# Scaled queries made in the transposed layout, the normalizer folded into the head LayerNorm, and the fill and the first loads moved

## The chip, the cores and the metric

The kernel runs on one core of a Trainium2 chip. The time is device microseconds of one execution, and the number compared is the median of several. A TensorE (PE) multiplies, a VectorE (DVE), a ScalarE (ACT) and a GpSimd (POOL) do the elementwise work, and a SyncE (SP) issues most DMAs. Each engine works through its own list in order, and they wait for each other on semaphores.

## The reference, cut to what matters

Input: `x` and `ctx`, 8 sequences of 512 tokens with 1024 features. Two residual blocks follow each other. The first is an mLSTM attention with 16 heads of 64, whose queries are the layer-normed x and whose keys and values are ctx. The second is a mixture of 16 experts, two per token, with a shared expert.

```python
log_D = log_fg + ig;  max_log_D = max over t;  D = exp(log_D - max_log_D)
C = (q @ k.T / sqrt(64)) * D
normalizer = maximum(abs(C.sum(-1)), exp(-max_log_D))
h = (C / (normalizer + 1e-6)) @ v
hn = (h - mean(h)) * rsqrt(var(h) + 1e-6) * ln_scale      # per head of 64
x1 = x + tanh(g_xattn) * hn
shared = (silu(f @ sg) * (f @ su)) @ sd                   # f: x1, layer-normed
routed = sum over the two best experts e of  w_e * (silu(f @ eg[e]) * (f @ eu[e])) @ ed[e]
out = x1 + tanh(g_ffn) * (shared + routed)
```

## The kernel before

The 4096 tokens are 32 chunks of 128, four to a sequence. There are two blocks, one after the other, with a barrier between them.

**The mix block** (`mix_block`) does, per chunk, both LayerNorms, gates, attention, router and the first half of the shared expert, whose weights stay in memory in a high and a low part (12 pieces, `w_hi` and `w_lo`, made from three staging slots in the first two turns: stage W). A chunk's work is cut into stages (a letter) and parts (a digit). One tuple, `TURN`, gives the order of all stages in a turn, and `OFFSET` says which chunk a stage works on: in the turn of chunk j, stage Q works on j+2, A (gates) and F on j+1, B (attention) on j, C (head LayerNorm) on j-1, D, E, N, G on j-2 and K, U, H, Y, J (shared expert) on j-3. Every engine runs the same tuple and takes from it the stages that it has. `AHEAD` is what comes ahead of the first turn. The first sequence is written out, six are a loop of four turns, and the last is written out with three turns more to drain.

Attention is chunkwise: within a chunk the scores times the decays (`gbd`, made from a row per head that goes to memory as `mid_g_row` and comes back to all 128 partitions), and across chunks a running `state` per head that is multiplied with scaled queries `qs_t`. In the three chunks of a sequence that have one ahead (j > 0), stage F makes `qs_t`: DVE multiplies the queries `q` by a factor per row and head (`qfac`, L674 and L676), PE transposes the product into `p_tr` (8 transposes of 128x128 in two halves, L850) and ACT copies each half out (L502). Stage Q makes the plain transposed queries `q_t` in the same way, from `q` (L626), through the same `p_tr`. Each half waits until the half ahead of it in `p_tr` has been copied out (`tr_before`).

Stage C divides the attention's output by the normalizer (L720 to L722), subtracts the mean per head and squares; the variance gets 1e-6 added (L731), and POOL takes its power -0.5 (L448).

**The expert block** (`ffn_block`) goes through the experts' tiles of 128 tokens (73 in this run), gathered by index, and then through the 32 chunks with the other half of the shared expert. A tile's output goes to `mid_y`, which has room for 98 tiles. The tiles beyond 73 are filled by SP with any finite rows, 25 DMAs from `mid_z` (L1139), between the second expert's weights and the first store of a tile (L1123). ACT can copy a tile's output into `y` (L1261) only when the store of the one before has landed. The last chunk gathers two rows per token (L1220, `r0` and `r1`), waits for them, joins them with the shared expert's half and stores 128 rows at once (L1132).

The kernel starts with seven constant loads, of which DVE, ACT and PE await all (`const_in` 112), then zeroes of the expert lists, then the first rows of x (L318).

## Time and profile before

| | us |
|---|---|
| median of 3 runs | 3263.84 (3263.45 to 3267.43) |
| the profiled execution | 3260.97 |
| its span, first to last instruction | 3259.4 |

| engine | busy us | share of the span |
|---|---|---|
| PE | 3012.4 | 92% |
| DVE | 1681.5 | 52% |
| ACT | 1025.7 | 31% |
| POOL | 609.4 | 19% |

The span has two parts: the mix block up to about 1326 us and the expert block behind it. Shares of the span are means over both, and DVE is busy at about 75 to 80% in the first and under 45% in the second. "Idle before" is the time that an engine stood still ahead of an instruction, and the name behind the arrow is what ended it. The 16 transposes of the plain and the scaled queries have one line, L850, with those of `xn` and `th`.

### The profile page before, as it was taken

The page shows a single profiled execution, that of the slowest core. Times are in us where ns is not written, and L with a number is a line of the kernel's source. Part 1 is how long each engine was busy: PE and PEld are TensorE (multiplying, and loading weights), DVE is VectorE, ACT ScalarE, POOL GpSimd, SP SyncE. Part 2 cuts the span into 40 slices and gives each one's busy share as a digit, 9 for nine tenths or more (in the row PEclk, how much of TensorE's full clock was granted, in tenths as well). Part 3 has the DMA queues.
Part 4 walks back from the last instruction along what each step waited for, and adds up shares of the span by engine and source line. Part 5 has one row for each costly group of instructions (what it writes and reads, how often), then busy time and mean ns, then how long its engine had stood idle before and what let it go on. Part 6 is the DMA issues. An engine that isn't in the chain of part 4 may idle for free.

```text
span 3259.4 us, 50815 instructions
## 1 busy us (share of the span) xinstructions
PE 3012.4 (92%) x17478; PEld 2478.7 (76%) x17479; DVE 1681.5 (52%) x3164; ACT 1025.7 (31%) x1940; POOL 609.4 (19%) x572
## 2 busy tenths in 40 slices
PE   3799998898989998689999999999999999999998
PEld 3677777777777776578888888888888888888886
DVE  3687777787878775323333333333333334444444
ACT  3444443343444331223233333333333321111110
POOL 1233333333333432100000000000000001111111
PEclk9699999999999997799999999999999999999999
DMA  4333333333434321553333442443242234444444
GB/s 151 117 105 121 115 119 116 105 105 107 126 108 123 111 85 46 216 179 140 135 136 135 142 173 103 174 161 114 101 175 100 109 135 152 145 154 137 157 146 133
DMA packets 200706, 424.54 MB, mean 130 GB/s; under 512 B 85472, under 2 KB 85984, under 8 KB 200160
## 3 DMA queue, kind: packets, MB, share of 16 engines
q1 hardware_dynamic: 176160, 349.67, 31.8%
q0 software_dynamic: 24400, 72.96, 6.8%
q8 instruction: 87, 1.43, 0.2%
q14 instruction: 59, 0.48, 0.0%
HBM read 333.42 MB, written 102.27 MB: 134 GB/s over the span
## 4 chain that ended last, share of the span: by engine, by line
PE 54%; DMA 1%; DVE 1%; issue 1%; ACT 1%; SPq 1%; ACTq 0%; POOL 0%; POOLq 0%; DVEq 0%
PE p_g_b L1451 17%; PE p_up_b L1451 17%; PE p_y_b L1439 16%; PE p_x_b L1419 3%; PE p_h_b L1426 1%; DMA mid_y<-y_b 1%; DVE w_lo_b L1294 1%; ACT w_hi_b L1237 1%; SPq L1139 0%; DMA xg_b<-mid_xn,idx_b 0%; DMA r_b<-mid_y,slot_now_b 0%; ACTq L1103 0%; DMA idx_b<-mid_lists 0%; SPq L1138 0%; DVE r_b L1347 0%
## 5 line engine op out<-in xcount | busy, mean ns | idle before, releaser
L1310 DVE TENSOR_TENSOR ht_lo_b<-p_h_b,ht_hi_b 128x512 fp32r<-128x512 f32 x105 | 72.5, 691 | 557.4 <-ACT ht_hi_b L1249 553.4
L1451 PE MATMUL p_g_b<-w_hi_b,xt_hi_b 128*128 128x512 f32 x840 | 339.2, 404 | 20.3 <-DVE w_lo_b L1294 18.4
L1439 PE MATMUL p_y_b<-w_hi_b,ht_hi_b 128*128 128x512 f32 x840 | 336.9, 401 | 6.8 <-DVE ht_lo_b L1310 6.8
L1451 PE MATMUL p_g_b<-w_hi_b,xt_lo_b 128*128 128x512 f32 x840 | 328.9, 391 | 0.0
L1451 PE MATMUL p_up_b<-w_lo_b,xt_hi_b 128*128 128x512 f32 x840 | 328.7, 391 | 0.0
L1451 PE MATMUL p_up_b<-w_hi_b,xt_lo_b 128*128 128x512 f32 x840 | 328.5, 391 | 0.0
L1439 PE MATMUL p_y_b<-w_hi_b,ht_lo_b 128*128 128x512 f32 x840 | 328.1, 391 | 0.0
L1451 PE MATMUL p_up_b<-w_hi_b,xt_hi_b 128*128 128x512 f32 x840 | 328.0, 391 | 0.0
L1439 PE MATMUL p_y_b<-w_lo_b,ht_hi_b 128*128 128x512 f32 x840 | 327.9, 390 | 0.0
L1451 PE MATMUL p_g_b<-w_lo_b,xt_hi_b 128*128 128x512 f32 x840 | 326.8, 389 | 0.0
L1322 DVE SCALAR_TENSOR_TENSOR sg_b<-th_b,p_g_b 128x512 f32<-128x512 f32 x105 | 72.2, 687 | 486.6 <-ACT th_b L1279 486.6
L1294 DVE TENSOR_TENSOR w_lo_b<-stage_b,w_hi_b 128x1024 fp32r<-128x1024 f32 x204 | 234.7, 1220 | 110.2 <-ACT w_hi_b L1244 66.9
L1249 ACT ACTIVATE ht_hi_b<-p_h_b 128x512 fp32r<-128x512 f32 x105 | 62.9, 599 | 558.2 <-PE p_h_b L1426 414.7
L919 PE MATMUL p_g<-w_hi,xt 128*128 128x512 f32 x512 | 221.9, 433 | 15.6 <-issue 14.4
L1190 POOL DMA_INDIRECT xg_b<-mid_xn,idx_b x73 | 71.1, 974 | 827.3 <-PE p_x_b L1419 785.4
L1279 ACT ACTIVATE th_b<-p_g_b 128x512 f32<-128x512 f32 x105 | 63.3, 603 | 512.9 <-PE p_up_b L1451 512.9
L919 PE MATMUL p_up<-w_hi,xt 128*128 128x512 f32 x512 | 209.1, 408 | 0.0
L1451 PEld LDWEIGHTS p_g_b<-w_hi_b,xt_hi_b 128*128 128x128 f32 x840 | 158.1, 188 | 55.6 <-DVE w_lo_b L1294 20.4
L1439 PEld LDWEIGHTS p_y_b<-w_hi_b,ht_hi_b 128*128 128x128 f32 x840 | 158.4, 189 | 36.9 <-DVE ht_lo_b L1310 7.4
L1451 PEld LDWEIGHTS p_g_b<-w_lo_b,xt_hi_b 128*128 128x128 f32 x840 | 158.0, 188 | 34.5
L1451 PEld LDWEIGHTS p_g_b<-w_hi_b,xt_lo_b 128*128 128x128 f32 x840 | 158.0, 188 | 34.2
L1451 PEld LDWEIGHTS p_up_b<-w_lo_b,xt_hi_b 128*128 128x128 f32 x840 | 157.7, 188 | 34.3
(216 smaller groups left out, 5837.5 us busy)
## 6 DMA issues: line engine op xcount, KB each, us to landing
mid_y<-y_b SPq DMA_DIRECT2D x73, 512.0 KB, 3.3
x<-in_x SPq DMA_DIRECT2D x64, 512.0 KB, 3.7
gbd<-mid_g_row SPq DMA_DIRECT2D x64, 512.0 KB, 5.1
stage_b<-in_eg SPq DMA_DIRECT2D x16, 2048.0 KB
stage_b<-in_eu SPq DMA_DIRECT2D x16, 2048.0 KB, 15.2
stage_b<-in_ed SPq DMA_DIRECT2D x16, 2048.0 KB, 19.4
ctx_t<-in_ctx_t SPq DMA_DIRECT2D x32, 512.0 KB, 4.6
ctx_v<-in_ctx SPq DMA_DIRECT2D x32, 512.0 KB, 7.7
```

Of the source, the lines that this page charges most:

```text
L919: last = nc.tensor.matmul(out[:, :], xt[:, a, k, :], w[:, k, o:o + FE], start=(k == 0 and m == 0), stop=(k == KD - 1 and m == 2))
L1190: nc.gpsimd.indirect_dma_start(out=xg[:, :], out_offset=None, in_=t["xn"], in_offset=bass.IndirectOffsetOnAxis(ap=idx[:, :], axis=0)).then ...
L1237: nc.scalar.activation(w_hi[:, p, :], stage[:, p, :], ACT.Copy).then_inc(gu_hi, 1)
L1249: nc.scalar.activation(ht_hi[:, :, :], p_h[:, :, :], ACT.Copy).then_inc(ht_hi_rdy, 1)
L1279: nc.scalar.activation(th[:, :], p_g[:, :], ACT.Tanh, scale=0.5).then_inc(tanh_rdy, 1)
L1294: nc.vector.tensor_tensor(w_lo[:, p, :], stage[:, p, :], w_hi[:, p, :].bitcast(f32), ALU.subtract).then_inc(sem_lo, 1)
L1310: nc.vector.tensor_tensor(ht_lo[:, :, :], p_h[:, :, :], ht_hi[:, :, :].bitcast(f32), ALU.subtract).then_inc(ht_rdy, 1)
L1322: nc.vector.scalar_tensor_tensor(out=sg[:, :], in0=th[:, :], scalar=1.0, in1=p_g[:, :], op0=ALU.add, op1=ALU.mult).then_inc(silu_step, 1)
L1419: last = nc.tensor.transpose(p_x[k // 4][:, k % 4, :], xg[:, k * P:(k + 1) * P], ident[:, :])
L1426: last = nc.tensor.transpose(p_h[:, k, :], h[:, k * P:(k + 1) * P], ident[:, :])
L1439: last = nc.tensor.matmul(p_y[n][:, :], a[:, k, :], b[:, GUP + k, w], start=(k == 0 and m == 0), stop=(k == FE // P - 1 and m == 2))
L1451: mm = nc.tensor.matmul(out[:, :], a[:, k, :], w[:, k, o:o + FE], start=(k == 0 and m == 0), stop=(k == KD - 1 and m == 2))
```

## The change

1. Stage F no longer multiplies and transposes q. DVE's row of log factors (`rows[:, 3]`, 16 heads by 128 tokens) is stored to memory (`mid_s_row`, 8 KB) by SP, comes back in two DMAs as factors that stand in the transposed layout (`qs_t`, 128 partitions by 8 by 128), ACT takes the exponential in one pass over `qs_t`, and DVE multiplies it with `q_t` and 1/8 in one pass. PE has no stage F, and one row fewer to transpose in A5.
2. The division by the normalizer n goes: the variance of the undivided output gets 1e-6 n² in place of 1e-6, which gives the same quotient.
3. The fill of `mid_y` goes to the mix block. As the number of tiles isn't known there, all 34 spare tiles are filled from rows of x, one DMA a chunk (stage D on SP) and two in the first turn.
4. The rows of x are the first load; ln_scale, the two gates, the lists' zeroes and two fills go to a new stage P in the first turn. The start waits for four constants. ACT's tanh and scaling go to P too. The 12 weight pieces have a fourth slot, and the shared expert waits piece by piece.
5. The last chunk of the expert block gathers its rows into free staging memory as soon as the weights are split, and stores its two halves apart.
6. `TURN` is another order: among others Q2 and Q3 have four parts of the gate and up products between them, A1 (the ctx_v load) comes behind A4 and E2 on SP, J1 ahead of N1 on DVE.

```diff
-        TURN = ("K7", "A1", "U1", "D1", "W1", "K8", "A2", "H1", "B0", "A3", "E1", "Y1", "B2", "A4", "E2", "Y2", "W2",
...
+        TURN = ("U1", "K7", "K8", "A2", "D1", "H1", "B0", "A3", "P1", "E1", "Y1", "A4", "E2", "A1", "B1", "Y2", "B2",
...
 # SP
+            def stage_d(part, b, j):
+                sp.dma_start(y_spare[c], x_rows[c]).then_inc(fill_in, 16)
...
                 if part == 4:
+                    if j > 0:
+                        ge_apart(sp, past, (sf_in, 32 * scaled_before(b, j)))
+                        sp.wait_ge(rows_rdy, c + 1)
+                        sp.dma_start(t["s_row"], rows[:, 3, :]).then_inc(s_out, 16)
...
+            def stage_f(part, b, j):
+                if part == 1 and j > 0:
+                    ge_apart(sp, past, (u_ps, NG * c))
+                    sp.wait_ge(s_out, 16 * n + 16)
+                    for o in range(2):
+                        sp.dma_start(qs_t[DH * o:DH * o + DH, :, :], s_rows[o].partition_broadcast(DH)).then_inc(sf_in, 16)
 # ACT
-                    nc.scalar.activation(qs_t[:, 4 * n:4 * n + 4, :], p_tr[:, :, :], ACT.Copy).then_inc(qs_sb, 1)
+                if part == 2 and j > 0:
+                    act.wait_ge(sf_in, 32 * n + 32)
+                    nc.scalar.activation(qs_t[:, :, :], qs_t[:, :, :], ACT.Exp).then_inc(sx_rdy, 1)
 # DVE
-                    link(nc.vector.tensor_scalar(qfac[:, :], cols[:, j, 3, :], DH ** -0.5, None, ALU.mult))
-                    dve.wait_ge(q_ps, 2 * c + 2)
-                    nc.vector.tensor_tensor(q[:, :, :], q[:, :, :], qfac[:, :, None].to_broadcast([P, NH, DH]),
+                if part == 3 and j > 0:
+                    dve.wait_ge(sx_rdy, scaled_before(b, j) + 1)
+                    nc.vector.scalar_tensor_tensor(out=qs_t[:, :, :], in0=qs_t[:, :, :], scalar=DH ** -0.5,
+                                                   in1=q_t[:, j % 2, :, :], op0=ALU.mult, op1=ALU.mult).then_inc(qs_sb, 1)
...
-                    link(nc.vector.reciprocal(nrm[:, 1, :], nrm[:, 0, :]))
-                    link(nc.vector.tensor_tensor(u, u, nrm[:, 1, :, None].to_broadcast([P, NH, DH]), ALU.mult))
+                    step(nc.vector.scalar_tensor_tensor(out=nrm[:, 1, :], in0=nrm[:, 0, :], scalar=H_EPS, in1=nrm[:, 0, :],
 # the expert block, SP
-            with sp.Fori(start(sp, NE), MAX_TILES) as f:
-                sp.dma_start(t["y"][bass.ds(f * P, P), :], base_rows[0]).then_inc(fill_in, 16)
...
+            for n in range(2):
+                half = slice(512 * n, 512 * n + 512)
+                sp.wait_ge(last_z, n + 1)
+                sp.dma_start(z_rows[NCH - 1][:, half], y[:, half]).then_inc(z_out, 16)
 # the expert block, POOL
-                gather(c - 1, c)
+                ge_apart(pool, past, (gu_split, GUP * (NE + 1)))
+                fetch(c - 1, c, slot_last, tuple(zip(last_r, last_in)))
```

On PE, in a looped turn before, behind the state's product and the router (`p_small<-rw`): `q` is the query tile, `p_g` and `p_up` the gate and up products.

```order
L850 MATMUL p_tr<-ident,q 128x128 [waits xl_sb,qs_rdy]
L850 MATMUL p_tr<-ident,q 128x128 x3
L39 REGISTER_ALU [waits qs_rdy]
L850 MATMUL p_tr<-ident,q 128x128 [waits qs_sb]
L850 MATMUL p_tr<-ident,q 128x128 x3
L919 MATMUL p_g<-w_hi,xt 128x512
...
L39 REGISTER_ALU [waits q_rdy]
L850 MATMUL p_tr<-ident,q 128x128 [waits qs_sb]
L850 MATMUL p_tr<-ident,q 128x128 x3
L39 ISA [waits q_rdy]
```

The same place now, with the products that stand between the two halves, and the first that follows the second half.

```order
L894 MATMUL p_tr<-ident,q 128x128 [waits xl_sb,q_rdy]
L894 MATMUL p_tr<-ident,q 128x128 x3
L957 MATMUL p_g<-w_hi,xt 128x512
...
L1043 MATMUL p_small<-hot,upper 128x16 [waits hot_rdy]
L1044 MATMUL p_small<-hot_acc,ones 128x16
L40 ISA [waits q_rdy]
L894 MATMUL p_tr<-ident,q 128x128 [waits q_sb]
L894 MATMUL p_tr<-ident,q 128x128 x3
L957 MATMUL p_g<-w_hi,xt 128x512
```

The four groups of transposes have become two, and the second has 24 products and the rank ahead of it and 12 (K7 and K8) ahead of the gates that read its result.

On ACT, in the same turn before, from the second half of `xt` on: the 16 exponentials of the decays `gbd`, then the copies out of `p_tr`, then the square of stage C.

```order
L510 ACTIVATE xt<-p_tr 128x512 [waits xn_ps]
...
L533 ACTIVATE gbd<-gbd,cols 128x128 [waits gb_rdy,cols_rdy]
...
L558 ACTIVATE ew<-ew 128x1 [waits top_rdy]
...
L502 ACTIVATE qs_t<-p_tr 128x512 [waits qs_ps]
...
L494 ACTIVATE q_t<-p_tr 128x512 [waits q_ps]
...
L494 ACTIVATE q_t<-p_tr 128x512 [waits q_ps]
...
L552 ACTIVATE sq<-uc 128x1024 [waits cen_rdy]
```

And now:

```order
L552 ACTIVATE xt<-p_tr 128x512 [waits xn_ps]
L543 ISA
L544 ACTIVATE qs_t<-qs_t 128x1024 [waits sf_in]
L571 REGISTER_ALU
L575 ACTIVATE gbd<-gbd,cols 128x128 [waits gb_rdy,cols_rdy]
...
L602 ACTIVATE ew<-ew 128x1 [waits top_rdy]
...
L538 ACTIVATE q_t<-p_tr 128x512 [waits q_ps]
L593 REGISTER_ALU
L596 ACTIVATE sq<-uc 128x1024 [waits cen_rdy]
...
L538 ACTIVATE q_t<-p_tr 128x512 [waits q_ps]
```

The wait for a DMA (`sf_in`) stands ahead of the 16 exponentials and of both query copies.

On SP, the turn now, from the row store on:

```order
L374 DMA mid_s_row<-rows 16x128 [waits rows_rdy]
...
L383 DMA gbd<-mid_g_row 128x1024 [waits c_rdy]
...
L399 DMA mid_xn<-xn 128x1024 [waits xn_rdy]
...
L369 DMA ctx_v<-in_ctx 128x16x64
L391 ISA [waits u_ps]
L393 DMA qs_t<-mid_s_row 64x8x128 [waits s_out]
L393 DMA qs_t<-mid_s_row 64x8x128
...
L335 DMA ctx_t<-in_ctx_t 128x1024
```

The factors' load waits for the attention's last product of the turn (`u_ps`) and has three loads and stores of 512 KB ahead of it in SP's list.

## Rows read from the trace of the kernel before

**Rows 1.** The page's first line.

```profile
span 3259.4 us, 50815 instructions
```

**Rows 2.** Stretches: length, busy of each engine, granted clock, DMA share, GB/s.

```profile
600.00:700.00 100.00, 90.05 (x684) 72.38 (x685) 77.07 (x179) 37.81 (x86) 35.10 (x23) 0.98 0.36 111
1415.00:1430.00 15.00, 7.16 (x23) 5.69 (x23) 3.17 (x5) 3.30 (x7) 2.11 (x3) 0.54 0.57 202
1400.00:3000.00 1600.00, 1574.91 (x7431) 1304.05 (x7430) 587.63 (x735) 469.61 (x689) 146.53 (x211) 1.00 0.39 138
```

**Rows 3.** What PE waited for, 200 to 1200 us: total, times, longest.

```profile
PE p_tr L850 <- DVE th L811: 29.5, 26, 1.2
PE p_tr L850 <- ACT qs_t L502: 22.1, 21, 1.4
PE p_tr L850 <- ACT q_t L494: 18.2, 26, 0.8
PE p_g L919 <- issue: 14.4, 5, 3.6
```

**Rows 4.** PE in order of time, 664 to 680 us: start, length, instruction, idle before.

```profile
664.89 1.15 PE L986 MATMUL p_u<-ctx_v,ks 128*64 128x65 f32 x32
...
670.95 0.66 PE L850 MATMUL p_tr<-ident,q 128*128 128x128 f32 x4
672.98 0.66 PE L850 MATMUL p_tr<-ident,q 128*128 128x128 f32 x4 [1.37 <-ACT qs_t L502]
...
679.45 0.29 PE L1003 MATMUL p_small<-hot,upper 128*128 128x16 f32 x2
```

**Rows 5.** Groups by line, 200 to 1200 us: busy, mean ns, idle before.

```profile
L747 DVE TENSOR_TENSOR x<-x,sq 128x1024 f32<-128x1024 f32 x27 | 32.7, 1212 | 0.0
L552 ACT ACTIVATE sq<-uc 128x1024 f32<-128x1024 f32 x26 | 27.5, 1059 | 48.8 <-DVE uc L726 48.8
L502 ACT ACTIVATE qs_t<-p_tr 128x512 f32<-128x512 f32 x42 | 25.0, 596 | 18.8 <-PE p_tr L850 18.8
```

**Rows 6.** ACT in order of time, from 665 us.

```profile
665.49 4.93 ACT L533 ACTIVATE gbd<-gbd,cols 128x128 f32<-128x128 f32 x16
```

**Rows 7.** DMA issues of 600 to 750 us: count, KB each, us to landing.

```profile
gbd<-mid_g_row SPq DMA_DIRECT2D x8, 512.0 KB, 5.3
ctx_v<-in_ctx SPq DMA_DIRECT2D x4, 512.0 KB, 7.9
```

**Rows 8.** DVE in order of time, 8 to 12 us.

```profile
8.91 0.42 DVE L599 TENSOR_TENSOR w_gate<-w_gate,state 128x256 f32<-128x256 f32 x1 [4.80 <-DMA gx<-in_g_ffn]
10.95 0.69 DVE L614 BATCH_NORM_STATS2 st<-x 128x6 f32<-128x512 f32 x1 [1.40 <-DMA x<-in_x]
```

**Rows 9.** PE in order of time, 68 to 82 us (the first turn's end).

```profile
71.23 1.11 PE L850 MATMUL p_tr<-ident,q 128*128 128x128 f32 x4 [3.44 <-DVE q L676]
79.85 1.08 PE L888 MATMUL p_small<-q_t,w_gate 128*32 128x128 f32 x16 [1.52 <-DMA ctx_t<-in_ctx_t]
```

**Rows 10.** SP, DVE and ACT in order of time, 1371 to 1425 us.

```profile
1372.10 23.60 SPq L1139 DMA_DIRECT2D mid_y<-mid_z  x25
1377.84 0.69 DVE L1322 SCALAR_TENSOR_TENSOR sg_b<-th_b,p_g_b 128x512 f32<-128x512 f32 x1 [4.81 <-ACT th_b L1279]
1395.55 0.69 DVE L1322 SCALAR_TENSOR_TENSOR sg_b<-th_b,p_g_b 128x512 f32<-128x512 f32 x1 [4.81 <-ACT th_b L1279]
...
1422.45 0.60 ACT L1261 ACTIVATE y_b<-p_y_b 128x512 f32<-128x512 f32 x1 [25.58 <-DMA mid_y<-y_b]
1424.67 0.68 DVE L1322 SCALAR_TENSOR_TENSOR sg_b<-th_b,p_g_b 128x512 f32<-128x512 f32 x1
```

**Rows 11.** PE, DVE and SP in order of time, 3242 to 3260 us.

```profile
3242.41 14.26 SPq L1132 DMA_DIRECT2D out<-y_b  x2
3248.01 0.39 PE L1439 MATMUL p_y_b<-w_lo_b,ht_hi_b 128*128 128x512 f32 x1
3250.82 0.75 DVE L1334 TENSOR_SCALAR r_b<-r_b,wts 128x1024 f32<-128x1024 f32 x1 [8.21 <-DMA r_b<-mid_y,slot_now_b]
```

More of the change, by code:

```diff
@@ L27 @@
 CAP = T
+SPARE = MAX_TILES - 2 * T // P
 PIECES = 12
@@ L30 @@
 NEG = -3.0e38
-DVE_PER_BATCH = 154
-SLOTS = 3
+DVE_PER_BATCH = 147
+SLOTS = 4
 def ge(eng, sem, n):
@@ L291, in tr_before @@
                         continue
-                if stage == "F" and where[1] == 0:
-                    continue
                 return tr_done(stage, part, *where)
@@ L300, in tr_done @@
                 return q_sb, 2 * c + part - 1
-            if stage == "F":
-                return qs_sb, 2 * turned_qs(b, j) + part - 1
             if stage == "N":
@@ L346, in stage_w @@
                         piece_in(p)
-                elif isinstance(b, int) and b == 0 and j < 2 and 6 * j + part - 1 + SLOTS < PIECES:
-                    piece_in(6 * j + part - 1 + SLOTS)
+                elif isinstance(b, int) and b == 0 and j < 2:
+                    for p in range(SLOTS, PIECES):
+                        if wp_last(p) == 6 * j + part - 1:
+                            piece_in(p)
             def stage_a(part, b, j):
@@ L898, in stage_a @@
                     ge_apart(pe, past, (rows_rdy, c + 1))
-                    which = [r for r in range(4) if not (r == 1 and j == CPB - 1) and not (r == 3 and j == 0)]
+                    which = [r for r in range(3) if not (r == 1 and j == CPB - 1)]
                     for r in which:
```

195 lines of the change are left out of this document (113 added, 82 removed).

## The prediction

> **What bounds the kernel now.** I read the page's head first: 3259.4 us from first to last instruction [rows 1] in an execution of 3260.97 us, 1.6 us around the span, with PE busy 92%. Then the stretches. In 1400 to 3000 us PE is busy 1574.91 of 1600 us at clock 1.00 [rows 2]. That is the expert block at its limit, and nothing of the change takes work from PE there. What can move lies in the mix block (up to 1326 us), at the border of the blocks and at both ends. So next I asked what PE waits for from 200 to 1200 us, the steady part of the mix block. The list is short [rows 3]: 29.5 us for `th` (stage U), 22.1 us for the scaled queries' copy out of `p_tr`, 18.2 us for the plain queries' copy, 14.4 us of the loop's return ("issue", 5 times). Together that is 84.2 of 1000 us, and 26 chunks pass in that time. PE is the bound of a turn, then, and the waits on `p_tr` are its second largest loss. 600 to 700 us shows the same from the other side: PE busy 90.05, DVE 77.07, ACT 37.81, DMA share 0.36 [rows 2]. In the first turns, where there is little to overlap, a chain of latencies sets the pace.
>
> **Stage F leaves PE.** A chunk with j > 0 has two groups of four transposes of the scaled queries. Each takes 0.66 us, and between the two PE stands 1.37 us until ACT has copied the first [rows 4]. The steady part has 21 such chunks (ACT's 42 copies [rows 5]). Waits: 22.1 us over 21 chunks [rows 3], 1.05 us each. Busy: two groups at 0.5 us, which is between 0.4 (the part in which no other product runs) and 0.66. Both go for 24 chunks: 24 x 1.05 = 25 us and 24 x 1.0 = 24 us, 49 us in all (44 to 57). The row that A5 no longer turns is under 0.1 us a chunk and I leave it out.
>
> **Q2 and Q3 are pulled apart.** Now Q3 stands behind four parts of the products, and the gates behind K7 and K8. The 18.2 us over 26 chunks, 0.70 each, had an ACT copy of 0.6 us as their cause. With over 5 us of products between the halves, the copy is hidden if ACT is there in time (below). 32 x 0.70 = 22 us. The 29.5 us for `th` and the 14.4 us of the loop stay: U1 still follows K8 directly, and nothing shortens the loop.
>
> **What stage F costs elsewhere.** DVE loses two passes of 128x1024 (L676 and L722), the factor's instruction and a reciprocal, and gains one such pass. L747, of the same shape, takes 1.212 us [rows 5]. DVE was not the bound and gets lighter by 1.2 us a turn or more. ACT loses two copies of 0.596 us and gains one pass of 128x1024: its square at 1.059 us is the nearest row [rows 5]. Even. The normalizer's fold changes nothing else; it is worth nothing by itself, since PE waits neither for L722 nor for what follows it.
>
> The price is the order on ACT. Exp over `qs_t` waits for a DMA and stands ahead of the 16 exponentials (4.93 us [rows 6]), which stand ahead of both query copies. I walk through one new turn from the end of the attention's last product, call it 0. SP then issues the two loads, 0.4 to 0.8 us each. Their landing isn't in the trace. The nearest rows are `gbd`, also a row from memory spread over all partitions, 5.3 us, and `ctx_v`, in pieces of 256 B, 7.9 us [rows 7]. The new load is in pieces of 512 B, nearer to `gbd`, but three transfers of 512 KB were issued ahead of it: I take 5.3 us. Exp starts at 5.3 and ends at 6.4, the 16 exponentials end at 11.3, the copy of Q2 at about 12. On PE the same time holds N2, G1, the state's product, the router, G2, Q2 and G3 to G6 with the rank. Before, 14.6 us pass from the state's product to the rank [rows 4], with five G parts, the router and all four groups in between. Without the groups and their waits (four of 0.5 us, 1.4 and 0.7 us, and half a us for q) 10 us remain. With the sixth part at 1.4 (six products), N2 and Q2 at 0.5 each and the rank at 0.3 it is 12.7 us. Q3 finds its place free with 0.7 us to spare. ACT then does C's square (1.1) and the copy of Q3, some 2 us ahead of the gates' need. So the forecast is no wait, but with a margin of half a us. At `ctx_v`'s 7.9 us it is 2.6 - 0.7 = 1.9 us late in each of 24 turns, 46 us. From both sides: 0 to 46 us; a gain is excluded, since the wait is new. I take 5 us, near the end that the nearer row gives.
>
> Two rules of the Trainium skill bear on that load. The rows say 5.3 us for two halves of `gbd` split by heads, each over all partitions [rows 7]. "DMA: Bandwidth & Descriptors", section "Rules for kernel authors", advises against two transfers to disjoint partition halves, as this one is, because they run on the same engines one behind the other. By that rule the split costs a second issue and brings nothing; no run here shows it yet, and the sum would change by less than 1 us a turn. The same page, "Latency and other measured facts", puts the latency of memory at 0.2 us on average and 2 us at high load. As an estimate by that page, 1.8 us more would make the load late by 1.1 us, 26 us over 24 turns. The DMA share of 0.36 [rows 2] doesn't look like high load, so the sum stays with the row.
>
> **The fill.** SP issues 25 fills in 23.60 us and then the first store of a tile, which sits behind them: ACT waits 25.58 us for it, to 1422.45 [rows 10]. What it costs is read from DVE's L1322, once per tile: 17.71 us from 1377.84 to 1395.55, then 29.12 us to 1424.67 [rows 10]. That is 11.4 us more. The next tile runs on a clock that fell during the stop (0.54 on average from 1415 to 1430 us, between the levels of 1.2 and 2.4 GHz [rows 2]): some 2 us more. All of it goes: 13 us (11 to 14). In the mix block come 34 fills. The old ones moved 25 in at most the 50.4 us from 1372.10 to 1422.45, 2.0 us each [rows 10]; now they come one in a turn of a stage whose DMA share is 0.36 [rows 2], and each is issued behind X1 and half a turn ahead of the row's store. I take nothing; the upper bound is a quarter of one fill in each of 32 turns, 16 us. The expert weights that the fill had beside it landed ahead of their use anyway.
>
> **The start.** DVE waits until 8.91 for the last of the seven constants, then until 10.95 for x [rows 8]. Now x is first and the four constants end with what was issued fourth: about 7 us. x is there by then, and the first statistics start at about 8 in place of 10.95: 3 us (2 to 4).
>
> **The first turns.** From F2 at 71.23 to the gates at 79.85 [rows 9] runs a chain of F2, F3, q, Q2 and Q3, at half clock and without other work, in each of two turns. Without F it is one group and one wait shorter for each half, and q doesn't wait for F's transposes: 6 us a turn, of which 2.1 are counted above. Two turns: 8 us. The weight pieces can start earlier with a fourth slot; stage P puts 2.3 MB ahead of the first factors, and a tanh with its table on ACT. No row prices either; I set them against each other, with as much as the chain itself on both sides: 7 us (-1 to 15).
>
> **The end.** The last product ends at 3248.4, and DVE waits 8.21 us for the gathered rows, to 3250.82 [rows 11]. Then come 5.5 us of joining and a store of 2.7 us that is issued at 3256.7. Now the rows are there, the scaling is done ahead of the product, and the first half is joined and stored while the second is computed. From 3248.4 follow 1.5 us for the second half and 3 us for its store: 3253. 6 us (4 to 7).
>
> **Sum.** 49 + 22 - 5 + 13 + 3 + 7 + 6 = 95 us off 3260.97: 3166 us for an execution like the profiled one. The median of the runs is 2.9 us above it, so 3169 us, 3% faster. The likeliest case's own range, with each term at its bounds but the load's at 0 to 1 us a turn, is 3145 to 3190.
>
> **Rivals.**
> A: the factors arrive late and ACT is the bound. For it: the wait has only 0.7 us to spare, and everything of ACT's turn hangs behind it. Against it: ACT is busy only 37.81 of 100 us [rows 2], and `gbd` lands in 5.3 us. Time: 46 us instead of 5, 3210 us (3190 to 3235).
> B: slower. The same mechanism, with the load queued behind fill, ctx_v and the xn store so that it needs 10 us or more. Then a turn is 10 - 5.3 - 0.7 = 4.0 us longer, in 24 turns 96 us, and the fills lie in that queue too, 16 us. The 5 us that I took fall away: 3169 - 5 + 112 = 3276 us. It decides from about 9.5 us to landing on. Against it: `ctx_v`, in the smallest pieces of all, needs 7.9 [rows 7].
> C: more than forecast. Where Q3 and F no longer break PE's flow, the wait for `th` shrinks too, since DVE is lighter: half of 29.5 us per 26 chunks, 18 us over 32 chunks, and the first turns bring their 15: 3143 us. For it: DVE's stage A2 moved ahead of D1. Against it: `th` needs one ACT pass and two DVE passes behind K8 in any order.
> D: the change doesn't take the waits off PE. The p_tr chain is the same with fewer links, and a wait for `th`, `xn` or the router's turn takes the freed time, because DVE between U1 and B1 has about as much to do as PE beside it. Then the busy part goes and half of the waits of 25 and 22 us stay: 24 us less, 3193 us. That falls together with the low side of A.
>
> **How the numbers follow.** The forecast 0.56, A and D together 0.26, C 0.12, B 0.06 with its neighbourhood. Below 3135 and above 3215 I leave out some 0.15: the range is 3135 to 3215. About 0.2%, 6.5 us, is what a measurement can tell from no change. All cases but B are faster by more than that; of B's 0.06 a third ends within: faster 0.93, same 0.02, slower 0.05.
>
> **What would show it.** Right: PE's waits have no L502 and almost nothing for `q_t`; a group of four turns is some 9 us shorter; the first store of a tile lands in 3 us and DVE's 17.7 us rhythm isn't broken; the first statistics are at 8 us; ACT waits for the DMA ahead of Exp for some us, yet is back before Q3. Wrong: PE waits for `q_t` by more than 1 us a turn, or for the gates; the load lands after 7 us or more; `ks` or the first decays of a turn are late. The sum would be wrong above all if the new order of `TURN` opens a wait that I walked past.

## The result, and the profile after

The changed kernel takes 3246.71 us (median of 4 runs, 3243.86 to 3251.57), the kernel before 3263.64 (3263.08 to 3267.43) on the same chip. The ratio is 0.9952, with a 95% interval of 0.9938 to 0.9967. So it is faster, by 0.5%, where 3% were forecast (3169 us), and the time lies outside the range of 3135 to 3215. The profiled execution of the changed kernel is the slowest of its four, 3251.57 us, 4.9 above the median; the one before is 2.7 below its own. So lengths that are compared between these two traces are too long for the changed kernel by some 7.5 us in all.

The two halves of the program went opposite ways. First DVE's first instruction of the expert block, which marks the border (columns here and in every timeline: start in us, duration in us, engine, line, operation, in brackets the idle time before it and its releaser), in the kernel before and then in the changed one:

```profile
1326.72 0.17 DVE L1362 MEMSET ones_b<- 128x128 f32 x1 [3.21 <-PEq L76]
```

```profile
1338.09 0.17 DVE L1418 MEMSET ones_b<- 128x128 f32 x1 [3.22 <-PEq L77]
```

In these traces the mix block is 11.4 us longer (the forecast had it 76 us shorter: 95 less fill and end). From the border to the end of the span it was 1932.7 us and is now 1911.9: 20.8 us shorter, where 13 and 6 were forecast.

What TensorE waits for from 200 to 1200 us in the changed kernel (total us, times, longest), to be held against [rows 3]:

```profile
PE p_tr L894 <- ACT q_t L538: 77.3, 20, 6.0
PE p_tr L894 <- DVE th L854: 24.6, 21, 1.8
PE p_g L957 <- issue: 8.5, 5, 2.4
```

The wait for the copy of the scaled queries (22.1 us) is gone as forecast. But the wait for the plain queries' copy, which was to go from 18.2 us to nearly nothing, is 77.3. The same question asked of ACT says why:

```profile
ACT qs_t L544 <- DMA qs_t<-mid_s_row: 181.7, 20, 11.1
```

ACT stands 9.1 us, in the mean of twenty turns, for the row factors' load. One of them in full, first SP's queue, then ACT, then PE:

```profile
664.38 0.36 SPq L399 DMA_DIRECT2D mid_xn<-xn  x1
665.10 0.62 SPq L369 DMA_DIRECT2D ctx_v<-in_ctx  x1
665.95 5.60 SPq L393 DMA_DIRECT2D qs_t<-mid_s_row  x2
671.74 0.48 SPq L335 DMA_DIRECT2D ctx_t<-in_ctx_t  x1
```

```profile
666.61 0.60 ACT L552 ACTIVATE xt<-p_tr 128x512 fp32r<-128x512 f32 x1 [0.23 <-PE p_tr L894]
677.70 1.06 ACT L544 ACTIVATE qs_t<-qs_t 128x1024 f32<-128x1024 f32 x1 [10.48 <-DMA qs_t<-mid_s_row]
678.66 4.76 ACT L575 ACTIVATE gbd<-gbd,cols 128x128 f32<-128x128 f32 x16
683.33 0.19 ACT L602 ACTIVATE ew<-ew 128x1 f32<-128x1 f32 x1
683.42 0.57 ACT L538 ACTIVATE q_t<-p_tr 128x512 f32<-128x512 f32 x1
```

```profile
678.44 0.37 PE L1044 MATMUL p_small<-hot_acc,ones 128*128 128x16 f32 x2
684.05 1.12 PE L894 MATMUL p_tr<-ident,q 128*128 128x128 f32 x4 [5.24 <-ACT q_t L538]
684.82 0.78 PE L957 MATMUL p_g<-w_hi,xt 128*128 128x512 f32 x1
```

The reader is to see four things. The pair of loads takes SP 5.60 us to issue, where two loads of `gbd` take 0.82. ACT gets the data 11.75 us after 665.95, not 5.3. All that follows on ACT follows at once, without a gap. And PE, after 5.24 us of nothing, runs four transposes in 1.12 us that took 0.66 in [rows 4], and a product in 0.78 that took 0.40 before the wait: the granted clock was 1.00 up to 682 us and 0.50 from 684 to 688. The windows show it on the large scale (us, busy time and instructions of PE, PEld, DVE, ACT, POOL, then granted clock, DMA share, GB/s), for the mix block before and after:

```profile
0.00:1326.70 1326.70, 1139.98 (x8656) 928.12 (x8657) 947.83 (x2225) 505.26 (x1170) 425.26 (x296) 0.95 0.35 108
```

```profile
0.00:1338.10 1338.10, 1120.10 (x8440) 917.02 (x8441) 913.56 (x2170) 492.83 (x1146) 403.51 (x296) 0.93 0.45 130
```

216 PE instructions fewer in the records, but only 19.9 us less of busy time, at a lower clock, and 31.3 us more of idle time (186.7 to 218.0).

### The profile page after: what moved, and what is told of

The parts are those of the page before. It is cut to its first block, busy times and chain, and to the rows that moved or that the text cites. A ratio compares the mean times of both kernels' runs of the same rounds, so it can differ in the third digit from the quotient of the medians.

```text
span 3250.0 us, 50376 instructions
## 1 busy us (share of the span) xinstructions
PE 2989.3 (92%) x17262; PEld 2465.7 (76%) x17263; DVE 1647.2 (51%) x3107; ACT 1013.8 (31%) x1916; POOL 588.7 (18%) x572
## 4 chain that ended last, share of the span: by engine, by line
PE 56%; DVE 1%; ACT 1%; issue 0%; DMA 0%; ACTq 0%; DVEq 0%; POOLq 0%
PE p_g_b L1506 18%; PE p_up_b L1506 18%; PE p_y_b L1494 16%; PE p_x_b L1474 3%; PE p_h_b L1481 1%; DVE w_lo_b L1344 1%; ACT w_hi_b L1287 1%; DMA xg_b<-mid_xn,idx_b 0%; ACTq L1145 0%; DMA idx_b<-mid_lists 0%; ACTq L1130 0%; DVE r_b L1400 0%; DVE sg_b L1372 0%; DVE r_b L1391 0%; ACT th_b L1329 0%
## 5 line engine op out<-in xcount | busy, mean ns | idle before, releaser
L1329 ACT ACTIVATE th_b<-p_g_b 128x512 f32<-128x512 f32 x105 | 63.3, 603 | 517.7 <-PE p_up_b L1506 517.7
L957 PE MATMUL p_up<-w_hi,xt 128*128 128x512 f32 x512 | 216.0, 422 | 0.0
L1506 PEld LDWEIGHTS p_up_b<-w_hi_b,xt_lo_b 128*128 128x128 f32 x840 | 157.9, 188 | 34.1
```

Of the source, the lines that this page charges most:

```text
L957: last = nc.tensor.matmul(out[:, :], xt[:, a, k, :], w[:, k, o:o + FE], start=(k == 0 and m == 0), stop=(k == KD - 1 and m == 2))
L1329: nc.scalar.activation(th[:, :], p_g[:, :], ACT.Tanh, scale=0.5).then_inc(tanh_rdy, 1)
L1506: mm = nc.tensor.matmul(out[:, :], a[:, k, :], w[:, k, o:o + FE], start=(k == 0 and m == 0), stop=(k == KD - 1 and m == 2))
```

## The experiments

"Before" in each is the kernel before, run beside it. "Mix block" is the time at which the marker above starts. Waits are those from 200 to 1200 us, and "landing" is the median time from a DMA's issue to its arrival. The steps that are moved: on ACT, F2 is the one pass over the loaded factors (the sixteen exponentials of the decays are A9, which follows it), and Q2 and Q3 are the copies of the two halves of the plain queries. On SP, F1 is the pair of factor loads, A1 the load of `ctx_v` and D1 the fill.

**1. The exponentials behind Q2 on ACT.** Edit, on ACT alone:

```
-  "R1", "F2", "A9", "A8", "S1", "B4", "Q1", "E3", "G2", "Q2", "G3",
+  "R1", "A9", "A8", "S1", "B4", "Q1", "E3", "G2", "Q2", "F2", "G3",
-  ge(act, qs_sb, scaled_before(b, max(j - 1, 0)) if j else (CPB - 1) * b)
+  ge(act, qs_sb, scaled_before(b, max(j - 1, 0)) if j else (CPB - 1) * b - 1)
```

> Edit: on ACT alone, the step F2 (wait for the loaded row factors, then their 16 exponentials) is moved from ahead of Q2 and Q3's copies to behind Q2, and the bound on the scaled queries for a batch's first chunk is one chunk looser. Everything else is the changed kernel. Theory ORDER (the load lands about 11 us after its release, and ACT's copies of q_t, for which TensorE waits 77.3 us over twenty turns between 200 and 1200 us, stand behind it in ACT's list): those waits go, and with what the clock gives back the kernel takes 3150 to 3190 us against 3247; the late load then shows as a wait on the scaled queries at most. Rival TRAFFIC (the load is late because the DMA queues are fuller, and they hold other stages up as well): the waits on q_t shrink but TensorE waits as long for th, for the gates or for the scaled queries, 3225 to 3250 us. Rival COVER (F2 behind Q2 delays the copy of Q3 and the scores): 3240 to 3270 us.

Measured: 3123.24 us, ratio 0.9576 (0.956 to 0.9592). The mix block ends at 1208.10. PE's waits:

```profile
PE p_tr L894 <- DVE th L854: 37.5, 30, 2.1
PE p_g L957 <- issue: 10.3, 5, 2.4
PE p_g L970 <- DVE ht L860: 4.6, 4, 1.4
```

`q_t` is no longer among them. (The expectation writes "their 16 exponentials" of F2; it is one pass.) The load itself is as late as it was (7.0 us from issue to landing, 7.1 in the changed kernel); only 48.4 us of ACT's wait are left, with nothing urgent behind it:

```profile
614.55 0.57 ACT L538 ACTIVATE q_t<-p_tr 128x512 f32<-128x512 f32 x1
617.57 1.06 ACT L544 ACTIVATE qs_t<-qs_t 128x1024 f32<-128x1024 f32 x1 [2.44 <-DMA qs_t<-mid_s_row]
618.53 1.04 ACT L596 ACTIVATE sq<-uc 128x1024 f32<-128x1024 f32 x1
619.52 0.60 ACT L538 ACTIVATE q_t<-p_tr 128x512 f32<-128x512 f32 x1
```

Theory ORDER holds and TRAFFIC falls: the queues are fuller (DMA share 0.50) and it doesn't matter. It brought 27 us more than the expectation's better end. The window says where that came from:

```profile
0.00:1208.10 1208.10, 1079.01 (x8440) 888.28 (x8441) 923.56 (x2170) 497.19 (x1146) 405.20 (x296) 0.95 0.50 144
```

Against the changed kernel PE is idle 88.9 us less (218.0 to 129.1), and the same 8440 instructions are busy 41.1 us less. The first is the wait. The second is for the most part what the clock gives back: PE's busy time in windows of 2 us, each times the part of the clock that was not granted in it, adds up to 72.8 us in the changed kernel and 37.0 here.

**2. The context values' load at the front of the turn.** Edit, on SP alone:

```
-  TURN = ("U1", "K7", ... "E2", "A1", "B1", ...
+  TURN = ("A1", "U1", "K7", ... "E2", "B1", ...
```

> Edit: on SP alone, the step A1 (load of the new context values, 2048 pieces of 256 B) goes from eight steps ahead of the row factors' load to the front of the turn, where the kernel before had it nearly. Theory QUEUE (the row factors' load lands late because the context values' load is ahead of it in the same queue: issued at 665.10, the factors' pair at 665.95, landed some 8 us later): the load lands 3 to 5 us after its issue, ACT's wait of 9.1 us a turn falls to 3 to 5 us, TensorE's wait on q_t from 77.3 to below 30 us between 200 and 1200 us, 3185 to 3215 us. Rival PIECES (the load is slow by its own 1024 pieces of 512 B): landing 6 to 7 us still, 3235 to 3250 us. Rival TRAFFIC (all queues are fuller): the same as PIECES here.

Measured: 3153.94 us, ratio 0.9673 (0.9655 to 0.969); the mix block ends at 1235.56. The time went further than theory QUEUE, whose wait on `q_t` holds (23.2 us), but whose landing of 3 to 5 us does not: it is 6.4 us, as rival PIECES had it, and ACT's wait is 126.0 us over 20 turns, 6.3 each. SP in one turn:

```profile
655.04 1.31 SPq L393 DMA_DIRECT2D qs_t<-mid_s_row  x2
656.48 0.54 SPq L335 DMA_DIRECT2D ctx_t<-in_ctx_t  x1
...
666.48 0.61 SPq L369 DMA_DIRECT2D ctx_v<-in_ctx  x1
667.34 3.42 SPq L330 DMA_DIRECT2D mid_y<-in_x  x1
```

The pair is issued in 1.31 us, and now it is the fill, which stands behind `ctx_v`, whose issue takes 3.42. The step of 2.8 us a turn on ACT (9.1 to 6.3) is the held issue and a little of the landing. PE waited 3.9 us a turn, and 1.2 are left (23.2 / 20).

**3. Pieces of 4 KB.** The row factors are stored as two blocks, so that every partition reads one piece of 4 KB instead of eight of 512 B:

```
-  s_rows = t["s_row"].rearrange("(k o) s -> o k s", o=2)
+  s_rows = t["s_row"].rearrange("(o k) s -> o k s", o=2)
-      sp.dma_start(t["s_row"], rows[:, 3, :]).then_inc(s_out, 16)
+      for o in range(2):
+          sp.dma_start(s_rows[o], rows[o:NH:2, 3, :]).then_inc(s_out, 16)
```

> Edit: the row factors are stored as two 8 x 128 blocks, even heads and odd heads apart, so that each partition of the load that spreads them reads one piece of 4 KB in place of eight of 512 B (128 pieces in all in place of 1024); one store more per chunk. Theory PIECES: the load lands 2 to 4 us after its issue, ACT's wait of 9.1 us a turn falls below 5 us, TensorE's wait on q_t below 30 us of 77.3, 3180 to 3215 us. Rival QUEUE (what is ahead in the queue sets it): landing still 6 us or more, 3230 to 3250 us. Rival BYTES (0.5 MB through the ring, however cut): the same 3240 to 3250 us.

Measured: 3264.09 us, ratio 1.001 (0.9996 to 1.0025). The load lands in 7.2 us and PE's wait on `q_t` is 87.3. PIECES falls: an eighth of the pieces, the same landing. The time is above both rivals' and 17 us above the changed kernel's. The second store is all that was added (in one turn the two take 1.40 us to issue, where one took 0.35); how it costs that, this run doesn't show.

**4. The fills back in the expert block.** The 34 fills are taken out of the mix block and put ahead of the first routed store. Its own time (3268.14 us, ratio 1.0025, 1.0011 to 1.0038) has that block's stall in it.

> Edit: the 34 fills of the spare rows leave the mix block; all of them stand ahead of the first routed store of the expert block, with a wait on them, so the expert block is longer than the kernel's before (a stall of 20 us or more there) and only the mix block's length is read: it ends at 1338.1 us in the changed kernel, 1326.7 in the kernel before. Theory FILLS (two fills a turn of 0.5 MB each, ahead in SP's queue, delay the other loads): the mix block ends at 1290 to 1315 us. Rival (the fills lie beside the work there, as the prediction priced them): it ends at 1333 to 1340 us.

The mix block ends at 1321.64, 16.5 us sooner than in the changed kernel, and a group of four turns is 153.9 us long in place of 156.4. PE's wait on `q_t` is 72.4, 4.9 less, so the wait alone is not all of the 16.5. The end lies between the two expectations: some of the lateness is the fills', most is not.

**5. The old mix block with the new expert block.**

```
+  def stage_d(part, b, j):                       # SP, kernel before
+      sp.dma_start(y_spare[c], x_rows[c]).then_inc(fill_in, 16)
```

> Edit: the mix block of the kernel before, with the 34 fills added to it (one a turn on SP at the step D1, two in the last places), followed by the changed kernel's expert block (no fill, the last tile's gather ahead, outputs in halves). It measures the moved fill and the end alone. Both traces so far give the expert block 20.8 us less (1932.7 to 1911.9 us). Theory SUM (the two parts are independent): 3238 to 3246 us, with the mix block ending at 1327 to 1332 us. Rival TRAFFIC (26 fills of 0.5 MB cost the mix block about what taking them out of the changed one gave back, 16.5 us): 3252 to 3262 us, mix block ending near 1343 us.

Measured: 3241.06 us, ratio 0.9933 (0.9916 to 0.9949), 21.8 us. The mix block ends at 1326.22 with the fills in it, 1326.72 without: there they are free. SUM holds. It is also faster than the whole change (3241.06 to 3246.71 us): the changed mix block was worth less than nothing.

**6. Both moves, 1 and 2.**

> Edit: the changed kernel with both moves: F2 behind Q2 on ACT (3123.2 us alone) and the context values' load at the front of the turn on SP (3153.9 us alone). Theory SAME CAUSE (both only free TensorE of the wait on q_t, of which 0 us is left with F2 late): 3118 to 3126 us. Rival SUM (the earlier load also takes away waits that F2 late leaves, POOL's on ctx_v above all, 54.1 us between 200 and 1200 us): 3095 to 3115 us. Rival BLOCKED TURN (A1 waits for the output products of the chunk before, and what SP issues behind it comes later): 3130 us or more.

Measured: 3122.3 us, ratio 0.9574 (0.9558 to 0.959); `q_t` is not among PE's waits. The intervals of 1 and 6 overlap: one cause, removed twice. These two are the fastest versions, 4.3% below the kernel before.

**7. The load on ACT's queue.** The pair is issued by ACT at F1's place in its own list, after the same waits.

```
-      sp.dma_start(qs_t[DH * o:DH * o + DH, :, :], ...).then_inc(sf_in, 16)
+      act.dma_start(qs_t[DH * o:DH * o + DH, :, :], ...).then_inc(sf_in, 16)
```

> Edit: the changed kernel's order, but the pair of loads that spreads the row factors is issued by ACT at the place of F1 in its own list (with the same two waits), on ACT's DMA queue, not SP's. Theory QUEUE (what delays the load is the work ahead of it in SP's queue, ctx_v's 2048 pieces and SP's blocked issue of up to 5.6 us): it lands 2.5 to 4.5 us after its issue of about 0.1 us on ACT, TensorE's wait on q_t falls from 77.3 to below 30 us between 200 and 1200 us, 3150 to 3200 us. Rival RING (all queues share the 16 engines and the delay is theirs): it lands 6 us or more after its issue still, 3235 to 3255 us. Rival ACT HELD (ACT, waiting for the store s_row to land before it issues, holds up its own copies): 3250 to 3290 us.

Measured: 3281.79 us, ratio 1.006 (1.0042 to 1.0078). Two rivals hold together, RING for the landing and ACT HELD for the time. ACT now stands ahead of the issue, and in the other waits of its list:

```profile
ACT cols L565 <- issue: 145.9, 20, 7.5
ACT qs_t L546 <- DMA qs_t<-mid_s_row: 47.0, 19, 4.2
```

The pairs themselves take 1.27 to 1.85 us to issue, 28.1 us for twenty; the rest of the 145.9, 5 to 6 us a turn, is the wait ahead of them, which in the turn at 679.20 is for the attention's last product on PE. What stands behind it on ACT comes later, and PE now waits 63.3 us for `decm` (the decay of the state) and 26.9 for `xt` in place of `q_t`. (The expectation laid ACT's standing on the store of the row; it had been issued 4.4 us earlier, at 674.79.)

The load still lands 7.5 us after its issue, from a queue with nothing ahead of it. So it is not the order in SP's queue that makes the landing 7 us. What does is seen in what the 16 DMA engines do meanwhile (last two columns: their share, GB/s). In the changed kernel, in the turn shown above:

```profile
662.00:664.00 2.00, 2.00 (x13) 1.69 (x13) 2.00 (x5) 1.72 (x5) 0.00 (x0) 1.00 0.04 8
664.00:678.00 14.00, 14.00 (x109) 12.00 (x108) 10.90 (x31) 2.15 (x5) 4.92 (x4) 1.00 1.03 259
678.00:680.00 2.00, 0.81 (x6) 0.62 (x5) 1.21 (x1) 2.00 (x6) 0.00 (x0) 1.00 0.08 31
```

They are full (the share can read above 1) from the issue of `gbd` until the factors arrive at 677.70, and nearly idle right behind it, though `ctx_t` and `mid_z` were issued only at 671.74 and 672.41: the factors arrive with the end of everything that was put in here. In each of the 20 turns between 200 and 1200 us the share is 0.73 to 1.05 in the last 2 us ahead of the arrival. In this experiment it is 1.24 from 683 to 689, up to the arrival at 689.12. How the engines divide their time among the transfers isn't shown. The landing of 7.5 us agrees with the Trainium skill, "DMA: Bandwidth & Descriptors", section "Issuing engines are not separate DMA queues": transfers of all issuers run on the same engines.

**8. As 1, with the fills in the expert block.**

> Edit: F2 behind Q2 on ACT as before (its mix block ends at 1208.1 us), and the 34 fills in the expert block instead of the mix block, with the wait on them; only the mix block's length is read. Theory COVERED (with TensorE's wait on q_t gone the fills lie beside the work, as the prediction had them, and they cost only as long as the factors' load decides): it ends at 1204 to 1210 us. Rival TRAFFIC (the fills delay other loads as well): 1188 to 1198 us.

The mix block ends at 1207.32, against 1208.10 with the fills. COVERED holds: what cost 16.5 us in experiment 4 costs 0.8 here, and a group of four turns keeps its length (138.1 to 137.9). The fills cost time only where PE hangs on the late load. (Its time, with the expert block's stall, is 3154.21 us, ratio 0.967, 0.9653 to 0.9687.)

**9. The kernel before with Q3 pulled apart from Q2.**

```
-  "G3", "Q2", "Q1", "X1", "Q3", "A7", "G4", "C1", "A8", "C2", "G5", "T1",
+  "G3", "Q2", "Q1", "X1", "A7", "G4", "C1", "A8", "C2", "G5", "Q3", "T1",
```

> Edit: the kernel before with one step of its turn moved: Q3 from right behind X1 (four of its steps behind Q2, none of them TensorE's) to behind G5, so that gate and up products stand between the two groups of query transposes. It prices one term of the forecast alone, the waits of Q3 on Q2's copy (-22 us). Theory TERM: 3238 to 3248 us, TensorE's wait on q_t from 18.2 to below 6 us between 200 and 1200 us. Rival CLOCK (a wait that goes lets the granted clock rise as well, so more than the wait comes back): 3215 to 3237 us. Rival HIDDEN (the wait moves to the next transposes, since one bank serves them all): 3255 to 3266 us.

Measured: 3238.92 us, ratio 0.9923 (0.99 to 0.9946), 25.8 us. `q_t` is gone from PE's waits. TERM holds: 22 us were forecast for this. One move in a list of names is worth more than the whole change as it stands.

**10. One load in place of two halves.** On top of the packed blocks of experiment 3:

```
-  for o in range(2):
-      sp.dma_start(qs_t[DH * o:DH * o + DH, :, :], s_rows[o].partition_broadcast(DH)) ...
+  sp.dma_start(qs_t[:, :, :].rearrange("p k s -> p (k s)"),
+      bass.AP(tensor=src.tensor, offset=src.offset, ap=[[KD * P, 2], [0, DH], [1, KD * P]])) ...
```

> Edit: the changed kernel with the row factors stored as two 8 x 128 blocks (as in the packed version, 3264.1 us, landing 7.2 us) and spread by one load over all 128 partitions, 0.5 MB, in place of two of 0.25 MB over 64 partitions each. Theory HALVES (a load that fills half of the partitions goes through fewer of what serves them): the load lands 4 to 5.5 us after its issue as gbd's 0.5 MB do (5.7), TensorE's wait on q_t from 87.3 to 40 us or less, 3190 to 3235 us. Rival QUEUE AND BYTES (0.5 MB behind ctx_v's 0.5 MB, however issued): lands 7 us or more, 3245 to 3268 us.

Measured: 3420.24 us, ratio 1.0473 (1.0449 to 1.0497), far outside both expectations. The load takes 17 us from its issue at 578.12:

```profile
578.12 3.99 SPq L394 DMA_DIRECT2D qs_t<-mid_s_row  x1
```

```profile
595.13 1.06 ACT L547 ACTIVATE qs_t<-qs_t 128x1024 f32<-128x1024 f32 x1 [16.85 <-DMA qs_t<-mid_s_row]
```

The Trainium skill gives a reason, in "DMA: Bandwidth & Descriptors", section "Why a DMA increments its semaphore by 16 and not by 1": the number of engines that share a transfer is the largest up to 16 that divides the slowest dimension of both sides, and my source's slowest dimension is 2. The trace agrees. In the last microseconds ahead of the arrival the share of the 16 engines is 0.12 to 0.14, which is two of them:

```profile
588.00:590.00 2.00, 1.88 (x11) 1.51 (x9) 0.00 (x0) 0.00 (x0) 1.26 (x1) 1.00 0.14 57
590.00:592.00 2.00, 0.00 (x0) 0.00 (x0) 0.00 (x0) 0.00 (x0) 0.00 (x0) 1.00 0.13 53
592.00:594.00 2.00, 0.00 (x0) 0.00 (x0) 0.00 (x0) 0.00 (x0) 0.00 (x0) 1.00 0.12 49
```

It is 0.12 or 0.13, at 49 to 53 GB/s, over the last 6 us ahead of the arrival in each of the 17 turns between 200 and 1200 us, and the loads issued behind it land late with it (`ctx_t` in 14.2 us, where the changed kernel has 6.9); as an estimate from these rows, 0.5 MB at that rate take some 10 us. No run here varied that dimension by itself. So this run says nothing on halves against one load of the same spread, which stays open.

**11. The exponentials just ahead of Q2.** Edit: F2 from ahead of A9 to between G2 and Q2, on ACT.

> Edit: the changed kernel with F2 on ACT moved from ahead of A9 to just ahead of Q2, so it is still ahead of both query copies, but the sixteen exponentials of the decay (4.8 us) and the steps A8 to G2 stand before the wait, not behind it. Theory ORDER AND AMOUNT (TensorE waits for what the load's lateness exceeds what ACT has to do before Q2; each turn's wait of 3.9 us is below the 4.8 us moved): TensorE's wait on q_t falls from 77.3 to 0 to 15 us between 200 and 1200 us, 3130 to 3160 us. Rival PLACE (any wait on the load ahead of Q2 holds the queries, and Q2 comes as soon as A9 ends): the wait stays above 40 us, 3190 us or more.

Measured: 3132.8 us, ratio 0.9591 (0.9568 to 0.9614). The wait is still ahead of both copies, but A9's 4.8 us now stand before it:

```profile
PE p_tr L894 <- ACT q_t L538: 7.6, 9, 1.8
```

77.3 to 7.6 us, as the arithmetic said. What matters is how much ACT does before the wait and how much after.

**12. Four loads of 32 partitions.**

```
-  for o in range(2): ... qs_t[DH * o:DH * o + DH, :, :], s_rows[o].partition_broadcast(DH)
+  for m in range(4): ... qs_t[32 * m:32 * m + 32, :, :], s_rows[m // 2].partition_broadcast(32)
```

> Edit: the changed kernel with its row factors spread by four loads of 0.125 MB over 32 partitions each in place of two of 0.25 MB over 64 (same bytes, same pieces of 512 B). So far two loads side by side landed in 7.1 us each and one of 0.5 MB over all partitions held ACT up to 17.6 us. Theory PER LOAD (each load moves at about 0.25 MB in 7 us by itself, and more of them share the work): each lands 3.5 to 5 us after its issue, TensorE's wait on q_t from 77.3 to 45 us or less between 200 and 1200 us, 3195 to 3235 us. Rival BYTES AND QUEUE (what is ahead and the 0.5 MB set the time): 7 us or more still, and SP's issues are blocked longer, 3245 to 3270 us.

Measured: 3239.16 us, ratio 0.9943 (0.9925 to 0.9962); PE's wait on `q_t` is 72.7 us and ACT's 177.2. Each load lands 4.1 us after its own issue, as PER LOAD has it, and next to nothing is won (ratio 0.9943, where the changed kernel has 0.9952), as BYTES AND QUEUE has it, because the issues are held:

```profile
581.02 0.61 SPq L369 DMA_DIRECT2D ctx_v<-in_ctx  x1
583.13 6.36 SPq L393 DMA_DIRECT2D qs_t<-mid_s_row  x4
589.67 0.36 SPq L335 DMA_DIRECT2D ctx_t<-in_ctx_t  x1
```

A landing that is counted from the issue leaves out what the issue waited.

## Why the prediction was wrong

**The step that failed** is "Their landing isn't in the trace. ... I take 5.3 us", in the part on the order on ACT. The walk around it was right. It gave 12.7 us from the last product of the attention to Q3's place; measured are 684.05 - 665.95 - 5.24 = 12.9. It gave 6.7 us from the load's arrival to the end of Q2's copy; measured are 683.99 - 677.70 = 6.3. With 11.75 us put in for 5.3, it says 11.75 - 5.3 - 0.7 = 5.7 us late, and 5.24 were measured in that turn. The mean of twenty turns is 77.3 / 20 = 3.9 us, 93 us over 24 turns, where the sum has "- 5"; with what the clock took on top, the late load cost 123.5 us (experiment 1).

**Why 5.3 was wrong.** [Rows 7] had two lines, `gbd` at 5.3 and `ctx_v` at 7.9. I chose by the size of the pieces. Experiment 3 shows that the pieces did not matter. What did: `ctx_v` goes right ahead of the load (experiment 2), whatever is issued next is held on SP (2, 12), and the fills add to it (4). And the load arrives only when the engines have done nearly all that the turn gave them (7). In the changed kernel the DMA (or pair) issued right behind `ctx_v`, whichever it is, took 3.38 to 6.23 us (median 5.26) in each of 25 turns between 200 and 1200 us. The trace of before could not show that: there the next issue behind `ctx_v` comes some 20 us later, and takes 0.32 to 0.34 us in 26 turns of 26. `gbd` was a poor neighbour for the same reason, since there SP had issued only a row of 8 KB in the 20 us ahead of it. A bound of 7.9 from `ctx_v`, counted from the issue, was too low by the held issue. What could have been seen is that the change puts `gbd`, the xn store, `ctx_v` and the factors, 2.5 MB, one behind the other in SP's list (issued from 663.38 to 665.95 in the turn shown), where before `gbd` and the store, 1.5 MB, stood by themselves. The text ahead of the prediction and the prediction count three transfers of 512 KB ahead of the factors; they are four, since `gbd` is two, each of 512 KB [rows 7]. And the share of 0.36, by which the prediction ruled out a high load, is a mean over 100 us. In one turn of the kernel before the engines are either nearly full or idle:

```profile
662.00:664.00 2.00, 1.93 (x19) 1.79 (x17) 1.81 (x7) 0.64 (x2) 0.55 (x1) 1.00 0.90 281
666.00:668.00 2.00, 2.00 (x14) 1.73 (x12) 1.97 (x4) 1.95 (x8) 1.15 (x2) 1.00 0.85 344
668.00:670.00 2.00, 2.00 (x16) 1.87 (x17) 2.00 (x1) 2.00 (x7) 1.81 (x1) 1.00 0.06 23
```

The new load was put into such a burst and not into the mean.

**Rival B** was this mechanism: the load queued behind fill, `ctx_v` and the xn store, decisive from 9.5 us on. It came true in its mechanism and not in its sign, because the other terms were larger than forecast. I gave it 0.06 and the milder rival A 0.26 shared with D; "`ctx_v`, in the smallest pieces of all, needs 7.9" was the argument against, and it was the wrong count. C and D fell: `th` is 37.5 us over 30 waits in experiment 1, about what it was [rows 3], and no other wait took the place of those freed.

**Stage F off PE: right, and too small.** The repeated group of four turns, read from the issues of `ctx_t`'s load on SP:

```
                       first repeated group   after five more   per group
before                        222.07              978.62          151.3
experiment 9 (Q3 apart)       221.66              960.15          147.7
changed                       202.93              984.91          156.4
experiment 1                  197.84              888.36          138.1
```

The forecast said "some 9 us shorter"; without the late load it is 13.2, of which 3.6 are Q2 and Q3 apart (2.8 in the forecast) and 9.6 stage F and the rest (6.1). Over the mix block PE is, in experiment 1, idle 57.6 us less than before and busy 61.0 us less. The waits were sized rightly; the busy part was entered at 24 us. Of the missing 37, some 9 are the transposes themselves: `p_tr<-ident,q` is busy 76.5 us before and 43.7 in experiment 1, 32.8 less, since a group takes nearer 0.66 us than the 0.5 that was entered. Some 11 are the clock: the sum over windows of 2 us, as in experiment 1, is 48.2 us before and 37.0 now (31.0 and 9.0 behind 200 us, 17.1 and 27.9 ahead of it). The other 17 are the same work in less time, and why isn't shown. The 512 products `p_g<-w_hi,xt` of the mix block, which the change doesn't touch, before and in experiment 1 (busy us, mean ns | idle):

```profile
L919 PE MATMUL p_g<-w_hi,xt 128*128 128x512 f32 x512 | 221.9, 433 | 15.6 <-issue 14.4 <-DVE x L825 1.2
```

```profile
L957 PE MATMUL p_g<-w_hi,xt 128*128 128x512 f32 x512 | 214.2, 418 | 10.3 <-issue 10.3
```

That is 7.7 us in one group of the same work. The prediction counted the clock for the expert block's stall and for no wait of the mix block, in either direction. Its range for the likeliest case has a slip too: with each term at its lower bound the sum is 44 + 22 - 24 + 11 + 2 - 1 + 4 = 58 us, which gives 3206 us and not 3190.

**The fill: right where it was taken from, wrong in its condition.** In the expert block the stop is gone; DVE's `sg_b`, one per tile, keeps its step of 17.7 us where [rows 10] had 29.12:

```profile
1406.68 0.69 DVE L1372 SCALAR_TENSOR_TENSOR sg_b<-th_b,p_g_b 128x512 f32<-128x512 f32 x1 [4.81 <-ACT th_b L1329]
1424.40 0.69 DVE L1372 SCALAR_TENSOR_TENSOR sg_b<-th_b,p_g_b 128x512 f32<-128x512 f32 x1 [4.81 <-ACT th_b L1329]
```

In the mix block the prediction says "I take nothing; the upper bound is a quarter of one fill in each of 32 turns, 16 us": measured are 0 to 0.8 us where no wait of PE hangs on the late load (5, 8), and 16.5 where one does (4).

**Start and end: right.** The statistics start at 8.57 in place of 10.95 [rows 8], 2.4 us for 3. At the end DVE waits 1.24 us for the last product and is done 1.5 us later, where [rows 11] has 8.21 us of waiting for rows and 5.5 of joining; from the last product to the end of the span pass 4.2 us in place of 11.0. The block as a whole gave 20.8 us against 19.

```profile
8.57 0.69 DVE L658 BATCH_NORM_STATS2 st<-x 128x6 f32<-128x512 f32 x1
```

```profile
3246.08 0.69 DVE L1400 TENSOR_TENSOR stage_b<-p_y_b,stage_b 128x512 f32<-128x512 f32 x1 [1.24 <-PE p_y_b L1494]
3246.80 0.75 DVE L1402 SCALAR_TENSOR_TENSOR y_b<-stage_b,tgf 128x512 f32<-128x512 f32 x1
```

**The first turns.** In the first turn, which [rows 9] shows at 71 to 80 us, Q3 meets the same late load (ACT stands 7.97 us for it, to 64.30):

```profile
70.65 1.08 PE L894 MATMUL p_tr<-ident,q 128*128 128x128 f32 x4 [9.12 <-ACT q_t L538]
```

Nevertheless the first repeated group starts 19.1 us earlier (202.93 for 222.07), 24.2 in experiment 1; start, first turns and a group's gain together were entered at 19.

**The account.** Relative to the kernel before: experiment 1 is 139 us faster. 21.8 of it are fill and end (5), about 25 are Q3 apart (9), the other 92 stage F, the start and the first turns, where 59 were entered for these; that split supposes that the parts add up. From experiment 1 to the changed kernel 123.5 us are lost by the medians; in the profiled runs it is 88.9 idle and 41.1 of slower busy time in the mix block. The forecast erred twice in opposite directions, by nearly 40 us too little and by nearly 120 too much.

What stays open: what share of the landing's 7 us belongs to which neighbour; why SP's issue is held behind `ctx_v`; whether one load spread as widely as the two halves would be quicker; and how the 92 us divide, since stage F alone was not put back.

## What to carry to other kernels

When a copy by an engine is replaced by a transfer, price it from its release to its arrival in the place where it will stand in the queue, the held issue included, and take the row of a neighbour there, not of the transfer that looks alike. Look at the DMA share in windows of a few us around that place, since a mean over many turns hides the bursts. Then count, in the list of the engine that waits for it, what stands behind the wait: the same late load cost 123 us in one place, 10 in the next (experiment 11 against 1) and nothing measurable in a third (1, where a landing 1.5 us sooner, in 6, changed nothing). And where waits of TensorE come or go, the products around them get slower or faster too: here about half as much again as the wait itself.

## What the runs showed of the hardware

- The DMA issued behind `ctx_v` (0.5 MB in 2048 pieces of 256 B) holds its issuer: 5.60 us for the pair of factor loads, 3.42 for the fill, 6.36 for four loads (in the turns shown), where the median issue takes 0.4. From 200 to 1200 us it is 3.38 to 6.23 us in the changed kernel (25 turns), 3.23 to 6.82 in experiment 1 (26), 2.15 to 4.04 in experiment 2 (26, the fill). No other DMA of these three takes over 1.9. In experiment 5 the fill stands there and takes 2.92 to 5.75 us (26 turns), in experiment 7 `ctx_t`, 4.45 to 6.58 (26). It follows the place, not the transfer.
- A broadcast load of 0.25 MB over 64 partitions landed in 6.4 to 7.5 us (5.5 in experiment 6), at 7.1 and 7.2 in pieces of 512 B and of 4 KB alike; of 0.125 MB over 32 partitions in 4.1; of 0.5 MB over 128 partitions by a source whose first dimension is 2, in some 17, on two of the 16 engines as the share of 0.12 to 0.14 says.
- The DMA engines work in bursts: in the changed kernel their share is 1.03 from 664 to 678 us and 0.08 behind it, where the mean over the mix block is 0.45. The factors arrive at its end. The mean of a stretch doesn't show it.
- ACT's own queue is no way around it: the load lands in 7.5 us, and ACT stands 145.9 us ahead of `cols` over twenty turns, of which 28.1 are the issues and the rest the wait ahead of them.
- After 5.24 us of waiting, four transposes of PE took 1.12 us, and 0.66 before the change, where they stood without such a wait [rows 4]; the granted clock was 0.50 behind the wait, from 684 to 688 us.
